# A block of attention and experts on one core: the queries' rotation halves are added on VectorE, GpSimd's batch in another order, normalised rows in other slots of ScalarE

## The reference

```python
h = _layernorm(x) * (1 + ca) + sa
# attention: per head
q, k = _rope(_rmsnorm(h @ wq)), _rope(_rmsnorm(h @ wk))
p = softmax(mask(q @ k.T / 128));  o = p @ (h @ wv)
x = x + ga * (o @ wo)
h = _layernorm(x) * (1 + cb) + sb
scores = softmax(h @ Wr + br);  _, top_idx = top_k(scores, 2)
x = x + gb * sum_over_two(weights * (gelu(h @ W1 + b1) @ W2 + b2))
# _rope(x): even, odd = split(x, 2)
#   concatenate([even * cos - odd * sin, even * sin + odd * cos])
```

## Time and profile before

| what | value |
|---|---|
| median of 3 runs | 1264.95 us (1257.93 to 1265.49) |
| the profiled execution | 1261.81 us |
| its span, first to last instruction | 1259.9 us |
| mean granted TensorE clock | 0.959 of full speed |
| busy share: PE, ACT, POOL, DVE | 84%, 78%, 74%, 66% |

### The profile page before, as it was taken

One profiled execution on the slowest core, in us unless ns is written; L12 is line 12 of the kernel. 1 busy time (PEld: TensorE's weight loads), 2 busy tenths in 40 slices (PEclk: granted clock), 3 DMA queues, 4 the chain that ended last, 5 costly groups with the idle time before them and its releaser, 6 DMA issues. The chain is left out here.

```text
span 1259.9 us, 30772 instructions
## 1 busy us (share of the span) xinstructions
PE 1063.7 (84%) x7431; PEld 797.9 (63%) x7431; DVE 826.7 (66%) x2489; ACT 979.9 (78%) x3518; POOL 935.0 (74%) x1326
## 2 busy tenths in 40 slices
PE   3689999999999999999999999999799668878700
PEld 2268787777777777777777777777655334467600
DVE  2776677766776666777666676776577456567544
ACT  3899998888888888888888888897599467777532
POOL 2887879879797797979779797988436656666533
PEclk9999999999999999999999999999999979999855
DMA  8300000000000000000000000000333232220074
GB/s 263 109 22 4 6 8 16 12 15 11 12 20 13 13 13 13 11 14 18 12 13 13 13 11 17 15 12 14 89 102 97 70 93 80 79 65 26 31 251 149
DMA packets 50820, 58.14 MB, mean 46 GB/s; under 512 B 7869, under 2 KB 38704, under 8 KB 50645
## 3 DMA queue, kind: packets, MB, share of 16 engines
q1 hardware_dynamic: 33492, 35.37, 9.4%
q0 software_dynamic: 8704, 16.87, 4.1%
q10 hardware_dynamic: 8448, 4.20, 1.1%
HBM read 33.21 MB, written 24.23 MB: 46 GB/s over the span
## 5 line engine op out<-in xcount | busy, mean ns | idle before, releaser
L544 POOL TENSOR_TENSOR roped<-roped,rope_b 128x512 f32<-128x512 f32 x256 | 331.1, 1294 | 80.0 <-DVE rope_b L1042 75.3
L724 ACT ACTIVATE squares<-unit 128x128 f32<-128x128 f32 x1024 | 272.8, 297 | 7.6 <-PE unit L1136 6.6
L1451 POOL DMA_INDIRECT y_rows<-y_out,place_y x144 | 156.6, 1088 | 114.3 <-DVE y_out L1833 70.3
L724 ACT ACTIVATION_READ_ACCUMULATOR squares<-unit 128x1 f32 x1024 | 232.4, 230 | 0.0
L1028 DVE TENSOR_TENSOR roped<-unit,cos_sb 128x512 f32<-128x512 f32 x256 | 175.8, 687 | 82.3 <-ACT squares L724 76.9
L700 ACT ACTIVATE probs<-scores,rr 128x256 f32<-128x256 f32 x256 | 123.2, 481 | 82.7 <-PE scores L1172 58.8
L1042 DVE TENSOR_TENSOR rope_b<-unit,sin_sb 128x512 f32<-128x512 f32 x256 | 174.5, 682 | 0.0
L1211 PE MATMUL unit<-ident,roped 128*128 128x128 f32 x1024 | 136.3, 276 | 27.6 <-POOL roped L544 14.0
L1211 PEld LDWEIGHTS unit<-ident,roped 128*128 128x128 f32 x1024 | 116.5, 141 | 64.7 <-POOL roped L544 21.6
L979 DVE RECIPROCAL den<-pv 128x2 f32<-128x2 f32 x256 | 41.7, 163 | 175.7 <-PE pv L1154 156.3
L995 DVE SCALAR_TENSOR_TENSOR acc<-pv,den,acc 128x128 f32<-128x128 f32 x448 | 136.7, 342 | 0.3
(11 more groups left out here) (292 smaller groups left out, 2917.6 us busy)
## 6 DMA issues: line engine op xcount, KB each, us to landing
shared<-y_rows SPq DMA_DIRECT2D x16, 512.0 KB, 5.5
x_all<-in_L_attn_x SPq DMA_DIRECT2D x32, 128.0 KB, 2.1
out_x<-sums ACTq DMA_DIRECT2D x16, 256.0 KB, 4.5
rope_b<-x_rows SPq DMA_DIRECT2D x13, 258.0 KB
tile_x<-x_rows SPq DMA_DIRECT2D x12, 258.0 KB
y_rows<-y_out,place_y POOLq DMA_INDIRECT x144
x_rows<-filler SPq DMA_DIRECT2D x16, 129.0 KB
k_t<-in_L_ffn_W SPq DMA_DIRECT2D x2, 1024.0 KB, 9.7
```

The lines of the kernel that those rows point to most:

```text
L544: pool.tensor_tensor(out=roped[parity][:, u, heads], in0=roped[parity][:, u, heads], in1=rope_b[:, u % 2, heads], op=ALU.add).then_inc(S[" ...
L724: nc.scalar.activation(squares[:, c * D:(c + 1) * D], UN[0][:, c * D:(c + 1) * D], ACT.Square, accum_out=ssq[parity][:, u * H + c:u * H + ...
L1451: pool.indirect_dma_start(out=y_rows, out_offset=bass.IndirectOffsetOnAxis(ap=place_y[i % (2 * SLOTS)][:, s:s + 1], axis=0), in_=y_out[at] ...
```

## The change

Four things change; all are in the first stage.

- The add of slots 0 to 3 (the queries) is no longer POOL's. DVE does it itself, in the same slot, behind its `rope_b`, and signals a semaphore of its own, `q_added`. POOL keeps the four adds of the keys.
- POOL's list of a step is in another order: `roots` stands first; both calls of `scatter` stand behind the second scaling, around `score`, and ahead of `h_lo` and of the keys' adds.
- On ACT, `xn` moves from slot 3 to slot 2, `xn2` from 6 to 3, and the routing's exponential `e_lg` from the end of slot 3 to slot 2, ahead of the copy of the values.
- The cast `TOP_F` is gone; `ONE_HOT` compares the integer indices themselves.

```diff
-        XN_AT, XN2_AT = 3, 6
+        XN_AT, XN2_AT = 2, 3
...
-            sp.wait_ge(S["add_done"], H * NB)
+            sp.wait_ge(S["add_done"], HH * NB)
+            sp.wait_ge(S["q_added"], HH * NB)
...
                 def scale_queries(t):
                     wait(pool, "rr_done", n + 2)
-                    wait(pool, "add_done", H * n)
+                    wait(pool, "q_added", HH * n)
...
-                if A:
-                    add(0)
                 if X or A or B or C or R or N2:
                     roots()
...
                 if B:
                     scale_queries(1)
-                if A:
-                    add(3)
+                now = ST and not (isinstance(n, int) and n - 6 == LAST - 1)
+                if now:
+                    scatter(0)
                 if RT:
...
+                if now:
+                    scatter(1)
                 if X:
                     b = n + 1
                     wait(pool, "hhi_done", b + 1)
...
+                    if RT and h == 2:
+
+                        b = n - 5
+                        wait(act, "route_step", STEPS * b + LESS_TOP)
+                        wait(act, "scored", b)
+                        nc.scalar.activation(e_lg[:], lg_m[:], ACT.Exp).then_inc(S["route_exp"], 1)
                     if B and h in VALUES:
...
-                    elif step == TOP_F:
-                        after(TOP_I1)
-                        ins = nc.vector.tensor_copy(top_f[:, :, :], top_i[:, :, 0:K])
...
                     if A:
-                        wait(dve, "add_done", w - 3)
+                        if h < HH:
+                            wait(dve, "add_done", HH * (n - 1) + h + 1)
                         nc.vector.tensor_tensor(
...
                                 .to_broadcast([P, HH, 2, D // 2]),
                             op=ALU.mult).then_inc(S["rope_done"], 1)
+                    if A and h < HH:
+
+                        wait(dve, "rope_done", w + 1)
+                        nc.vector.tensor_tensor(out=roped[parity][:, u, heads], in0=roped[parity][:, u, heads],
+                                                in1=rope_b[:, u % 2, heads], op=ALU.add).then_inc(S["q_added"], 1)
...
                         if u >= TT:
-                            wait(pe, "add_done", 2 * (NU * b + u + 1))
+                            wait(pe, "add_done", HH * b + 2 * (u - TT + 1))
```

More of the change, by code:

```diff
@@ L215, in adaln_block @@
         top_i = sb("top_i", [P, TT, 8], U32)
-        top_f = sb("top_f", [P, TT, K])
         gap = sb("gap", [P, TT])
@@ L243, in adaln_block @@
             split_done wvo_scaled wvo_hi_done tx_done p_done tr_done vw_done s_done o_done ht32_done
-            hhi_done h_ready sq_done ropea_done rope_done add_done qs_done tr_copied vals_ready exp_done
+            hhi_done h_ready sq_done ropea_done rope_done add_done q_added qs_done tr_copied vals_ready exp_done
             den_done acc_done x2_done stat_done mv_done chain_done guess_done newton_step rr_done off_done xn_ready router_in
@@ L292, in iterations @@
                 body(n // 2, n % 2, live(n))
-        (TOP_L0, TOP_L1, LESS_TOP, E_SUM, E_REC, TOP_S0, TOP_S1, TOP_I0, TOP_I1, TOP_F, ONE_HOT) = range(1, 12)
+        (TOP_L0, TOP_L1, LESS_TOP, E_SUM, E_REC, TOP_S0, TOP_S1, TOP_I0, TOP_I1, ONE_HOT) = range(1, 11)
         STEPS = ONE_HOT
@@ L585, in body @@
                     newton()
-                if A:
-                    add(1)
-                if X or A or B or C or R or N2:
                     offsets()
@@ L598, in body @@
                                        op=ALU.mult).then_inc(S["place_k_done"], 1)
-                if A:
-                    add(2)
                 if B:
                     scale_queries(1)
-                if A:
-                    add(3)
+                now = ST and not (isinstance(n, int) and n - 6 == LAST - 1)
+                if now:
+                    scatter(0)
                 if RT:
@@ L616, in body @@
                         .then_inc(S["h_ready"], 1)
-                now = ST and not (isinstance(n, int) and n - 6 == LAST - 1)
-                if now:
-                    scatter(0)
                 if ST:
@@ L628, in body @@
                     add(4)
-                if now:
-                    scatter(1)
-                if A:
                     add(5)
@@ L777, in body @@
                                                  bias=off[1 - parity][:, TT + t:TT + t + 1]).then_inc(S["xn2_done"], 1)
-                    if RT and h == 3:
-                        b = n - 5
-                        wait(act, "route_step", STEPS * b + LESS_TOP)
-                        wait(act, "scored", b)
-                        nc.scalar.activation(e_lg[:], lg_m[:], ACT.Exp).then_inc(S["route_exp"], 1)
                     if ST and h == 0:
@@ L838, in _ @@
                 (1, 0): (TOP_L0, TOP_L1), (1, 1): (LESS_TOP,), (3, 3): (E_SUM,), (3, 4): (E_REC,),
-                (5, 0): (TOP_S0, TOP_S1), (5, 1): (TOP_I0,), (5, 2): (TOP_I1,), (5, 3): (TOP_F,),
+                (5, 0): (TOP_S0, TOP_S1), (5, 1): (TOP_I0,), (5, 2): (TOP_I1,),
                 (6, 1): (ONE_HOT,)}
@@ L927, in route @@
                         ins = nc.vector.max_index(top_i[:, t, :], top_s[:, t, :], score[:, t, :])
-                    elif step == TOP_F:
+                    elif step == ONE_HOT:
                         after(TOP_I1)
-                        ins = nc.vector.tensor_copy(top_f[:, :, :], top_i[:, :, 0:K])
-                    elif step == ONE_HOT:
-                        after(TOP_F)
                         wait(dve, "place_k_done", b)
                         ins = nc.vector.tensor_tensor(
-                            out=one_hot[:, :, :],
-                            in0=iota_e[:, :].rearrange("p (o e) -> p o e", o=1).to_broadcast([P, TT * K, E]),
-                            in1=top_f[:, :, :].rearrange("p t (j o) -> p (t j) o", o=1)
-                                .to_broadcast([P, TT * K, E]), op=ALU.is_equal)
+                            out=one_hot[:, :, :].rearrange("p (t j) e -> p t j e", j=K),
+                            in0=iota_e[:, :].rearrange("p (a o e) -> p a o e", a=1, o=1).to_broadcast([P, TT, K, E]),
+                            in1=top_i[:, :, 0:K].rearrange("p t (j o) -> p t j o", o=1)
+                                .to_broadcast([P, TT, K, E]), op=ALU.is_equal)
                     ins.then_inc(S["route_step"], 1)
```

## The result

The changed kernel took 1267.67 us in the median of 20 runs (1261.53 to 1276.35), the kernel before 1261.03 us (1257.56 to 1267.09) in 20 runs on the same chip: a ratio of 1.005, with a 95% interval of 1.0032 to 1.0069. The forecast was 1235 us. In two later sets of runs, on two of the three chips on which the kernel before takes 1214 to 1217 us, the same changed kernel measured 0.973 and 0.975. "The profile after" is that of the first comparison; why the same kernel loses in one comparison and gains in others is what the experiments are about.

The account below looks back on a forecast made before the run. POOL was taken to pace the attention steps, with PE next once freed; ten pairs at 2.4 us (24 us) and seven further steps (6 us) gave -30 us, so 1235 us as median, range 1224 to 1246, chance 0.55.

Parts of the forecast that it names:

- POOL's order: POOL in a loop step: from the scatters' wait to the last keys' add takes 12 us against 15.6 on DVE.
- less than 1 us per pair: DVE's adds beside POOL's scatters: added blocked time if, against the expected rule, a scatter blocked DVE too.
- is not touched: The stage of the experts, from 900 us on, was claimed to be unaffected by the change.
- The sum: Whole kernel: -30 us, made of 24 us from ten pairs at a jump and 6 us from seven further steps.
- The short step is near 24 us: Expected sign in the attention loop: the short step, 24.9 us before, near 24 us, and the pair 52.3 us.
- Nothing of the change removes the jump: Long step of the loop: the jump's 4.9 us per pair was claimed to stay.
- The term for DVE's adds: Eight queries' adds per pair on DVE: 0.68 us each, 5.4 us, plus about 0.3 us each blocked by POOL, 2.4 us.
- DVE becomes the bound: Rival, chance 0.10: DVE's adds each lose 0.9 us to POOL, a pair is 2.4 us longer, 1297 us.
- The cast: DVE's top_f, 0.85 us on average, goes: 1.7 us per pair off DVE.
- PE's gain: PE's waits for POOL's roped and xn2 go: 1.9 to 3.7 us per pair, taken as 2.4.
- The floor is nearly reached: Rival, chance 0.17: all 3.7 us per pair go and seven steps gain 1.8 us each, 50 us, 1215 us.
- if the pair stays at 54.7 with POOL idle: One of the stated signs, in the attention loop, that the forecast is wrong; the pair was expected at 52.3 us.

Follow-up runs that it names:

- e13: Changed kernel with both scatter calls back behind h_lo and the first keys' add: 1236.71 us, 0.9844 of the kernel before (1254.95 us).
- e14: Changed kernel with only the second scatter call back behind the first keys' add: 1232.54 us, 0.9811 of the kernel before (1254.95 us).
- e7: Kernel before with only the scatters moved ahead of score and h_lo, all adds on POOL: 1331.09 us, 1.0556 of the kernel before (1264.02 us).
- e6: Kernel before with only the cast top_f gone, the compare reading integers: 1257.09 us, 0.995 of the kernel before (1264.02 us).
- e15: Changed kernel with the hardware loop written out, four stores in a row kept: 1197.81 us, 0.9534 of the kernel before (1254.95 us).
- c2: Kernel before, unchanged, run again for a trace on an on-time chip: 1214.49 us, 0.9997 of the kernel before (1214.98 us).
- c1: Changed kernel, unaltered, run again on an on-time chip: 1183.23 us, 0.9734 of the kernel before (1214.98 us).
- e4: Changed kernel with all 36 steps written out, no hardware loop, on an on-time chip: 1165.43 us, 0.9581 of the kernel before (1216.89 us).
- e1: Changed kernel with both scatter calls back behind h_lo and the first keys' add, on an on-time chip: 1186.91 us, 0.9755 of the kernel before.
- e5: Kernel before with all 36 steps written out, no hardware loop, on an on-time chip: 1179.78 us, 0.9701 of the kernel before (1214.98 us).
- e8: Kernel before with only ACT's new slots (xn, xn2, the exponential earlier): 1270.53 us, 1.0053 of the kernel before (1264.02 us).
- e2: Changed kernel with ACT's slots as before (xn, xn2, the exponential), on an on-time chip: 1191.1 us, 0.9793 of the kernel before (1216.89 us).

## Why the prediction was wrong

**The step that failed** is the one on POOL's order. The prediction costed the moved scatters as POOL's own time only ("it is four indirect stores at 0.99 us with 0.24 us of idle before each", 12 us against 15.6), and took their effect on other engines as nothing or "less than 1 us per pair" of blocked DVE. On POOL that working held: it waits for `place` up to 2.1 us a step, and PE no longer waits for its adds (8.1 us in the earlier trace rows, gone after). What it left out is what the other engines see while the four stores go out: in the first comparison's loop PE's signals came late by 162 us in sum, and some 2 us of that fell on the path of each step: PE waits 24.8 us for ACT's `q_t` in 14 steps, and `q_t` waits for the signal (570.75 and 570.78 in the place shown). By the traces the attention ended at 909.7 us, 6.0 later than in the kernel before (903.7); on the second chip it ended at 862.2 against 894.0, 31.8 earlier. The 37.8 us between the two are nearly the whole of the distance between forecast (-30 us) and the profiled result (+10.8). No rival had this mechanism, so no chance was given to it, and the slower side was put down to DVE alone.

On late chips the versions with the stores apart or back gain and have a quarter of the late signals (e13, e14 against the change), and moving the stores alone makes such signals (e7: 67, against 19 in e6 on the same chip). So on such a chip the order of the stores multiplies them; e15 against the first comparison says that in the changed kernel the loop has to be there too. What the stores and the loop do to PE's signals, and why only some chips show it, stays open: no run separates the stores' traffic from the loop's own work, and the changed kernel was not run beside e13 and e14, nor e7 on an on-time chip. What argues against the chip as the sole reason for the better ratios of e13 and e14 is that the kernel before takes 1255 to 1264 us in all three late cases, and that e7 and e6 differ on one and the same chip. That a kernel is "on time" on three chips and late on others was seen in one set on each, so whether it belongs to the chip or to the hour of the set is open too.

A sign of it could have been read in the kernel before. The prediction said that the experts' stage "is not touched" and did not read its waits. The list of waits of the kernel before, 905 to 1190 us, and the same of c2 over 895 to 1190:

```profile
DVE y_pos L1828 <- remote: 70.2, 14, 21.4
...
ACT hidden L1538 <- remote: 23.4, 15, 7.1
```

```profile
DVE y_pos L1828 <- PE y_turned L1958: 30.2, 31, 1.6
```

On the first chip DVE and ACT stand 94 us for "remote" there, beside POOL's indirect stores of `y_rows`; on the second chip the same waits go by PE's own name and the longest is 1.6 us. The stage takes 356 us on the one and 319 on the other. The change leaves it alone as forecast (361 and 319), so it is no part of the difference beyond 5 us, which one execution of each can't settle.

**What held, where signals are on time** (c1 against c2, each step of the working):

- The sum: 31.7 us by the two spans (1213.0 and 1181.3), forecast 30. Ten pairs gave 28.1 us, forecast 24; the other steps 3.6, forecast 6. The two misses nearly offset each other.
- "The short step is near 24 us" was wrong: 24.88 before, 25.08 after. I had read POOL as its bound; PE takes 24.84 us for a step even with the loop written out (e4), so nothing was to be had there. The earlier trace rows spoke against it: PE's 50.79 us in a pair are 25.4 a step. The gain is in the long step, where the distance to the short one fell from 4.4 to 1.0 us. "Nothing of the change removes the jump" was true of the jump, and false of its price.
- The term for DVE's adds was too small: 0.68 + 0.3 us each was taken, and 1.13 us is measured (1.146 in c1), with DVE's pair busy 45.2 against 43.9 us. By groups, 300 to 700 us of the profile after, against the earlier trace rows:

```profile
L1039 DVE TENSOR_TENSOR roped<-roped,rope_b 128x512 f32<-128x512 f32 x59 | 66.6, 1130 | 2.0
```

It is not chance how each add meets POOL: each slot's add meets the same operation in every step. Between 300 and 700 us of c1 the adds of slots 0 to 3 take 0.81, 2.07, 0.99 and 0.69 us on average, and no slot varies by more than 0.02. POOL's scaling and the add of slot 1 beside it, and the add of slot 3 beside the stores, in c1:

```profile
379.54 1.90 POOL L552 TENSOR_TENSOR roped<-roped,rr 128x1024 f32<-128x1024 f32 x1
...
379.90 2.08 DVE L1039 TENSOR_TENSOR roped<-roped,rope_b 128x512 f32<-128x512 f32 x1
...
386.92 0.69 DVE L1039 TENSOR_TENSOR roped<-roped,rope_b 128x512 f32<-128x512 f32 x1
```

The first stands until the scaling ends at 381.44 and then takes its 0.54 us. The one that starts during the indirect store of 386.02 to 387.06 takes 0.69 us, and in e1, where POOL has nothing under way when it starts, 0.69 too, in all 16 steps of each: it loses nothing. The Trainium skill infers the same (SBUF — State Buffer, "Who interferes with whom"), that building DMA descriptors leaves a DVE instruction with two inputs alone; here the traces agree. The prediction's proof of it, was none: there DVE's instruction had started first and could not be the one to wait, and the store took 1.28 us where the median of its kind is 0.99. DVE still has 2.5 to 3.4 us of slack per step in c1, and the rival "DVE becomes the bound" did not come: on the late chip too DVE is busy 22.6 of 26.9 us.

- The cast, taken as 1.7 us per pair off DVE, is worth 0.5% alone, on a late chip (e6).
- PE's gain was taken as 2.4 us per pair from a range of 1.9 to 3.7; it is 2.8. "The floor is nearly reached", 1215 us, needed 3.7 and did not come in the loop. It came only with the loop written out too: e4 is 51.5 us below the kernel before.
- I would be wrong "if the pair stays at 54.7 with POOL idle": so it was in the first comparison, though for a reason that I had not thought of.

## What to carry to other kernels

A move that frees an engine also moves its DMA issues, and these can cost other engines time that their own duration doesn't show; put "remote" or unnamed waits beside the issuing engine's timeline, in every stage and before forecasting. Compare on more than one chip before a change is called a gain or a loss: this one is 0.973 on one and 1.005 on another, while writing out the loop holds on both kinds (on-time 0.958 and late 0.953 with the change, late 0.960 with the scatters back). When two engines are near the bound, ask for the floor of the step first: here PE's busy time of a pair, 50.79 us or 25.4 a step, stood in the table and spoke against a step near 24 us; the pair came to 51.36 us, and to 49.68 with the loop written out.

## What the runs showed of the hardware that I had not expected

- PE's signals come up to 2.7 us late in the changed kernel's loop and 3.2 us in e7, and waits for "remote" reach 22 us in the experts' stage, in the first comparison and two sets, and in none of the three other sets. The kernel before takes 1255 to 1264 us there and 1214 to 1217 us in the others. Of the 47 us between the two traced, 37 lie in the experts' stage, where PE's signals that are over 0.3 us late sum to 220 us from 900 to 1200 us of the one trace, and the other has none; that they make the whole of it is not shown.
- On on-time chips a hardware loop over two steps costs 3.5 us per pair in the kernel before (54.17 against 50.65 us without the loop, c2 and e5, one chip) and 1.7 us in the changed one (51.36 against 49.68, c1 and e4, two chips). Writing out the loop is worth 3% before and 1.6% after.
- ACT's earlier slots alone cost 0.5% on a late chip (e8) and were worth some 0.4 to 0.6% on an on-time one beside the adds on DVE (0.9793 without them in e2; 0.9734 and 0.9754 for the whole change, on other chips).
